# Two attention and expert layers on one core: nine rank matmuls, expert row copies three tiles ahead, stored key parts in eight buffers, and a table zeroed in long rows

## The reference, cut to what matters

```python
x = x + tanh(g_xattn[0]) * _L0_xattn_ref(_layernorm(x), ctx, ...)   # additive attention, pooled queries and keys
x = x + tanh(g_ffn[0])   * _L0_ffn_ref(_layernorm(x), ...)
x = x + tanh(g_xattn[1]) * _L1_xattn_ref(_layernorm(x), ctx, ...)   # softmax attention, 16 heads of 8
x = x + tanh(g_ffn[1])   * _L1_ffn_ref(_layernorm(x), ...)

# _L0_ffn_ref: two of eight experts for each token
logits = flat_x @ W_router + b_router
top_vals, top_idx = jax.lax.top_k(logits, TOP_K)
router_weights = jax.nn.softmax(sparse_logits, axis=-1)
for e in range(NUM_EXPERTS):
    h = jax.nn.relu(flat_x @ W1[e] + b1[e])
    y = h @ W2[e] + b2[e]
    final_output = final_output + y * w[:, None]
```

## Time and profile before

| | |
|---|---|
| time, median of 3 runs | 921.75 us (920.45 to 923.25) |
| time of the profiled execution, its span | 925.03 us, 923.3 us |
| busy: TensorE, VectorE, ScalarE, GpSimd | 58%, 50%, 29%, 42% of the span |
| mean granted TensorE clock | 0.743 |
| chain that ended last | VectorE 28%, TensorE 28%, issue 11%, unknown 11%, DMA 8% |
| first expert gather, last expert matmul of layer 0 | about 259 and 421 us |
| first and last expert matmul of layer 1 | about 779 and 894 us |

### The profile page before, as it was taken

One profiled execution on the slowest core, in us unless ns is written; L12 is line 12 of the kernel. 1 busy time (PEld: TensorE's weight loads), 2 busy tenths in 40 slices (PEclk: granted clock), 3 DMA queues, 4 the chain that ended last, 5 costly groups with the idle time before them and its releaser, 6 DMA issues.

```text
span 923.3 us, 16362 instructions
## 1 busy us (share of the span) xinstructions
PE 535.6 (58%) x4815; PEld 434.2 (47%) x4816; DVE 459.1 (50%) x1520; ACT 265.5 (29%) x442; POOL 384.9 (42%) x436
## 2 busy tenths in 40 slices
PE   2588774313069898882455566564544002999980
PEld 2256562211058777782233455443433001988870
DVE  5674686544213332234973578777785620222224
ACT  1220011201023334343511366464544100232220
POOL 5121016655115555555000245256575571555660
PEclk9786785655569999997555578577655555999995
DMA  8999999923222222211463354332114112222218
GB/s 206 247 149 171 157 149 150 131 78 99 95 58 67 68 65 65 66 55 55 112 207 111 78 146 113 86 97 48 38 42 122 36 48 62 76 73 74 70 47 278
DMA packets 108712, 94.56 MB, mean 102 GB/s; under 512 B 12344, under 2 KB 97080, under 8 KB 108584
## 3 DMA queue, kind: packets, MB, share of 16 engines
q1 hardware_dynamic: 94584, 70.04, 36.9%
q0 software_dynamic: 9840, 21.60, 8.5%
q10 hardware_dynamic: 4224, 2.10, 0.8%
HBM read 46.15 MB, written 47.45 MB: 101 GB/s over the span
## 4 chain that ended last, share of the span: by engine, by line
DVE 28%; PE 28%; issue 11%; another core or an unknown queue 11%; DMA 8%; POOL 4%; SPq 4%; ACT 3%; DVEq 2%; POOLq 0%; ACTq 0%
PE PS L698 25%; DVE work L1205 4%; DMA work<-ys 3%; DVE stats L1210 2%; DVE XN L1228 2%; DVE work L1614 2%; DVEq L1528 2%; DVE rtmp L1205 2%; DVE X L1205 2%; POOL xs L461 1%; DMA k_parts<-work 1%; DMA q_parts<-w1l 1%; DVE nwt L1221 1%; DVE work L1534 1%
## 5 line engine op out<-in xcount | busy, mean ns | idle before, releaser
L698 PE MATMUL PS<-work 128*128 128x36 f16 (+6 forms) x1376 | 109.0, 258 | 95.4 <-DVE work L1205 70.4
L472 POOL DMA_INDIRECT ys<-work x144 | 144.4, 1003 | 34.5 <-issue 34.5
L698 PE MATMUL PS<-w,work 128*128 x1152 | 145.0, 279 | 10.5 <-issue 6.4
L698 PEld LDWEIGHTS PS<-w,work 128*128 128x128 f32 x1152 | 134.2, 192 | 21.8 <-issue 20.4
L698 PEld LDWEIGHTS PS<-work 128*128 128x128 f16 (+3 forms) x1376 | 87.9, 138 | 118.4 <-issue 80.9
L1205 DVE TENSOR_TENSOR work<-PS,work 128x128 f32<-128x128 f32 (+4 forms) x130 | 51.2, 415 | 175.6 <-issue 59.8
L497 POOL TENSOR_TENSOR work<-XN,work 128x1024 f16<-128x1024 f32 x32 | 68.0, 2126 | 162.9 <-ACT work L1149 162.6
L461 POOL DMA_INDIRECT xs<-pack,adr_i x96 | 93.9, 978 | 68.7 <-ACT pack L1053 38.6
L698 PE MATMUL PS<-work,w1h 128*128 128x256 f16 x576 | 102.5, 279 | 9.9 <-DVE work L1516 8.7
L1103 ACT ACTIVATE work<-PS,b 128x256 f32<-128x256 f32 x160 | 62.7, 474 | 110.8 <-PE PS L698 96.6
L698 PE MATMUL PS<-work,w1l 128*128 128x256 f16 x288 | 80.2, 279 | 0.3 <-issue 0.3
(11 more groups left out here) (238 smaller groups left out, 840.0 us busy)
## 6 DMA issues: line engine op xcount, KB each, us to landing
xs<-zrow SPq DMA_DIRECT2D x8, 2210.0 KB
work<-xs SPq DMA_DIRECT2D x144, 65.0 KB
work<-ys SPq DMA_DIRECT2D x16, 512.0 KB, 4.4
k_parts<-work SPq DMA_DIRECT2D x24, 128.0 KB
q_parts<-w1l SPq DMA_DIRECT2D x24, 128.0 KB
w<-k_parts SPq DMA_DIRECT2D x8, 384.0 KB
work<-q_parts SPq DMA_DIRECT2D x8, 384.0 KB
work<-k_parts SPq DMA_DIRECT2D x32, 96.0 KB
```

The source lines that it names most:

```text
L472: g.indirect_dma_start(ys[l], bass.IndirectOffsetOnAxis(xin[:, q, u, :].bitcast(U32)[:, D:D + 1], 0), yrow[:, q, u, :], None).then_inc(ff[ ...
L698: return t.matmul(o, lhsT, rhs, start=start, stop=stop, skip_group_check=True)
```

## The change

**Rank:** `route_rank` covers all 8 tiles with one output of 64 columns: the running count broadcast to all, then each shift by one tile over the columns that remain, then the triangle. That makes 1 + 7 + 1 = 9 matmuls, in both layers. **Copies ahead:** a round does parts(q+3) and then result(q), in both layers; in layer 0 the expert is read before the waits, on VectorE and on ScalarE. **Key parts:** `k16` has eight buffers, at another place in the work area, and ScalarE no longer waits for stores. The stores of chunks 4 to 7 are issued behind the loads of the first eight expert tiles, and the waits for all key stores move behind experts(0), on SyncE and on ScalarE. **Zeros:** GpSimd clears 16 rows in each partition inside `w2`, and SyncE writes the table from there in 17 DMAs of 8,320 bytes for a partition. `w2` is loaded once these have landed, with its own semaphore `w2_in`, for which TensorE waits.

```diff
+ZROWS = 16
+ZPARTS = E * CAP // (P * ZROWS)
+FILLED = 16 * (ZPARTS + 1)
+AHEAD = 3
-        k16 = at(0, [2, 2, CHUNK], F16)
+        k16 = at(28, [NC, 2, CHUNK], F16)
+        zrows = w2[:, 0:ZROWS * ROW16 // 2].bitcast(F16)
...
+            g.memset(w2[:, 0:ZROWS * ROW16 // 2], 0.0).then_inc(zero, 1)
...
-            sp.dma_start(w2[:].rearrange("p (e c d) -> p e c d", e=E, c=FC),
-                         A["w2_0"].rearrange("e (c p) d -> p e c d", p=P)).then_inc(w_late, 16)
-            sp.wait_ge(zero, 1)
-            for e in range(E):
-                sp.dma_start(xs[1][e * CAP:(e + 1) * CAP, :].rearrange("(p m) n -> p m n", p=P),
-                             bc(zrow[:].bitcast(U32), 1, CAP // P)).then_inc(filled, 16)
+            sp.wait_ge(zero, 2)
+            spread = xs[1][0:E * CAP, :].rearrange("(p a m) n -> p a (m n)", p=P, m=ZROWS)
+            for part in range(ZPARTS):
+                sp.dma_start(spread[:, part, :], zrows.bitcast(U32)).then_inc(filled, 16)
...
+            sp.wait_ge(filled, FILLED)
+            sp.dma_start(w2[:].rearrange("p (e c d) -> p e c d", e=E, c=FC),
+                         A["w2_0"].rearrange("e (c p) d -> p e c d", p=P)).then_inc(w2_in, 16)
...
-            for c in range(NC // 2, NC):
-                keys_stored(c)
-            for u in range(2):
-                sp.wait_ge(qk_out[u], PART_STORES * (NC // 2))
             sp.wait_ge(tails, 16 * E)
...
-                expert_tiles(sp, l, step)
+                for q in range(XS_LEAD):
+                    step(0, q)
+                if l == 0:
+                    for c in range(NC // 2, NC):
+                        keys_stored(c)
+                with sp.Fori(1, rounds[l]) as i:
+                    for q in range(XS_LEAD):
+                        step(i, q)
...
             y_load(0, 1)
+            for u in range(2):
+                sp.wait_ge(qk_out[u], PART_STORES * (NC // 2))
...
-                t0 = pair(p).start
-                for s in range(2 * CT_TILES):
-                    o = PS[:, BANK_RANK[l], RANK0 + s * E:RANK0 + (s + 1) * E]
-                    mm(o, ones16[:], cum16[:], stop=False)
-                    for b in range(s):
-                        mm(o, ones16[:], sel16[:, t0 + b, :], start=False, stop=False)
-                    ins = mm(o, tri16[:], sel16[:, t0 + s, :], start=False)
-                ins.then_inc(rt[l]["rank"], 1)
+                sel, n = sel16[:, pair(p), :], 2 * CT_TILES
+                o = PS[:, BANK_RANK[l], RANK0:RANK0 + n * E].rearrange("p (s e) -> p s e", e=E)
+                mm(o, ones16[:], bc(cum16[:], 1, n), stop=False)
+                for back in range(1, n):
+                    mm(o[:, back:n, :], ones16[:], sel[:, 0:n - back, :], start=False, stop=False)
+                mm(o, tri16[:], sel, start=False).then_inc(rt[l]["rank"], 1)
...
-                if l == 1:
-                    pe.wait_ge(w2_in, 16)
+                pe.wait_ge(w2_in, 16 * (l + 1))
...
-                        if c >= 2:
-                            act.wait_ge(qk_out[c % 2], PART_STORES * (c // 2))
...
+                    if l == 0:
+                        e = dve.value_load(eidx_i[0:1, l, ds(i * XS_LEAD + q, 1)], min_val=0, max_val=E - 1)
                     dve.wait_ge(f["y"][v], m + 1)
...
-                def round_(i, first, last):
+                def round_(i, last):
                     for q in range(XS_LEAD):
-                        if q < XS_LEAD - 1:
-                            parts(i, q + 1)
+                        if q + AHEAD < XS_LEAD:
+                            parts(i, q + AHEAD)
                         elif not last:
-                            parts(i + 1, 0)
-                        if q >= 1:
-                            result(i, q - 1)
-                        elif not first:
-                            result(i - 1, XS_LEAD - 1)
+                            parts(i + 1, q + AHEAD - XS_LEAD)
+                        result(i, q)
```

More of the change, by code:

```diff
@@ L351, in slots @@
             return tiles(c if l == 0 else c % 4)
-        NL = 4
+        NL = 3
         NW = 8
@@ L489, in _ @@
             experts(0)
-            pool.wait_ge(filled, 16 * (E + 1))
+            pool.wait_ge(filled, FILLED)
             for step in range(NT + 16):
@@ L1078, in _ @@
                         act.wait_ge(qk_ps, c + 1)
-                        act.wait_ge(soft["pooled"], 4)
-                        if c >= 2:
-                            act.wait_ge(qk_out[c % 2], PART_STORES * (c // 2))
-                        a.activation(k16[:, c % 2, 0, :], PS[:, BANK_K[c % 2], :], ACT.Copy).then_inc(qk_hi, 1)
+                        act.wait_ge(soft["head_prod"], 4)
+                        a.activation(k16[:, c, 0, :], PS[:, BANK_K[c % 2], :], ACT.Copy).then_inc(qk_hi, 1)
                 elif step == "choose":
@@ L1096, in step @@
                     v, m = q % 2, (i + i0) * (XS_LEAD // 2) + q // 2
+                    if l == 0:
+                        e = act.value_load(eidx_i[0:1, l, ds(i * XS_LEAD + q, 1)], min_val=0, max_val=E - 1)
                     act.wait_ge(f["up"][v], m + 1)
@@ L1100, in step @@
                     if l == 0:
-                        e = act.value_load(eidx_i[0:1, l, ds(i * XS_LEAD + q, 1)], min_val=0, max_val=E - 1)
                         for c in range(FC):
@@ L1120, in blanked @@
                              bc(zrow[:, 0:2 * D], 1, HG * HG * CHUNK // (2 * D)), ACT.Copy).then_inc(s_, 1)
+            for u in range(2):
+                act.wait_ge(qk_out[u], PART_STORES * (NC // 2))
             for u in range(2):
@@ L1485, in _ @@
                         dve.wait_ge(qk_hi, c + 1)
-                        tt(k16[:, c % 2, 1, :], PS[:, BANK_K[c % 2], :], k16[:, c % 2, 0, :], ALU.subtract)\
+                        tt(k16[:, c, 1, :], PS[:, BANK_K[c % 2], :], k16[:, c, 0, :], ALU.subtract)\
                             .then_inc(qk_lo, 1)
@@ L1527, in result @@
                     if l == 0:
-                        e = dve.value_load(eidx_i[0:1, l, ds(i * XS_LEAD + q, 1)], min_val=0, max_val=E - 1)
                         tt(yrow[:, q, :, :], y, bc(b2b[:, ds(e * D, D)], 1, 2), ALU.add).then_inc(f["biased"][0], 1)
@@ L1535, in result @@
                     ins.then_inc(f["yrow"][v], 1)
-                def round_(i, first, last):
+                def round_(i, last):
                     for q in range(XS_LEAD):
-                        if q < XS_LEAD - 1:
-                            parts(i, q + 1)
+                        if q + AHEAD < XS_LEAD:
+                            parts(i, q + AHEAD)
                         elif not last:
-                            parts(i + 1, 0)
-                        if q >= 1:
-                            result(i, q - 1)
-                        elif not first:
-                            result(i - 1, XS_LEAD - 1)
+                            parts(i + 1, q + AHEAD - XS_LEAD)
+                        result(i, q)
                 rounds_ = TILES[l] // XS_LEAD
-                parts(0, 0)
-                round_(0, True, False)
+                for q in range(AHEAD):
+                    parts(0, q)
+                round_(0, False)
                 with dve.Fori(1, rounds_ - 1) as i:
-                    round_(i, False, False)
-                round_(rounds_ - 1, False, True)
-                result(rounds_ - 1, XS_LEAD - 1)
+                    round_(i, False)
+                round_(rounds_ - 1, True)
             def combine(l, c):
```

2 lines of the change are left out of this document (1 added, 1 removed).

## The result

The changed kernel takes 912.04 us (median of 20 runs, 900.38 to 922.36), the kernel before, run beside it, 921.85 us (916.87 to 925.38). The ratio is 0.985, 95% interval 0.983 to 0.987: faster by 1.5%. Either way the time lies above the range of the prediction. The profiled execution took 915.8 us, its span is 914.0 us.

The account below looks back on a forecast made before the run. Layer 0's late routing was taken as bound by key-store waits and TensorE's slow rank instructions, experts(0) by copy order. Terms -17.3 - 21.5 - 9 - 16 = -63.8 us took the 921.75 us median to 858 us; range 843 to 886.

Parts of the forecast that it names:

- Nine matmuls in stage A: Layer 0's routing: nine rank matmuls remove VectorE's three waits, -21.5 us.
- the instructions past the first eighty: TensorE's ranks: instructions past the first eighty cost, not array work; nine matmuls, 18 instructions, stay well inside.
- Rival 1: Layer 0's ranks: slow steps have another cause, say GpSimd's scatters, and nine matmuls still meet them; 879 us, chance 0.12.
- the fast 40: Layer 0's rank: the first 40 of 44 matmuls ran fast, always at the start; held against rival 1.
- Stores off the path: Between last tail and first row load: moving stores of chunks 4 to 7 saves 17.3 us, bounds -12 to -17.5.
- up to 2 us of loss: Experts(0): twelve stores behind 16 row loads, some 6.5 us, might cost up to 2 us; in the bounds, not the sum.
- Layer 1's four ranks: Layer 1's routing: nine matmuls shorten waits before its four `route_rows`, -9 us, bounds -3 and -13.
- Copies three ahead: Experts(0): earlier copies remove the wait before up and most before down, -16 us, bounds -2 and -27.
- 4.00 us a tile: Experts(0): a tile takes 4.00 us; copies ahead would make it 3.60 over 40 tiles.
- Rival 2: Experts(0): relu's output or y banks become the next wait, 3.95 us a tile; 872 us, chance 0.17.
- The same order in experts(1): Experts(1): no copy wait to remove, result stands behind one more gather; 0 us, bounds -6 and +4.
- Zeros: Early table zeroing: long rows free the DMA queues earlier but bring 0 us, bounds -3 and +2.

Follow-up runs that it names:

- slow-step batches: Batches of executions in which the kernel before, unchanged, took 921.9 and 928.7 us; the prediction's profile is of this sort.
- `after`: The changed kernel against the kernel before, first measurement and its profile: 912.04 us, ratio 0.985.
- `rank_b`: The kernel before with nine rank matmuls in place of 44 and nothing else, in a slow-step batch: ratio 0.991.
- `before_b`: The kernel before, no edit, run again in a slow-step batch: 923.7 us.
- `stores_spread`: The changed kernel with one of the twelve late key-part stores behind each row load of tiles 8 to 19, slow-step batch: 906.95 us, 0.976 of the kernel before.
- even batches: Batches of executions in which the kernel before, unchanged, took 863 to 872 us.
- `after_b`: The changed kernel, no edit, run again in a slow-step batch: 917.61 us beside 928.73 for the kernel before, ratio 0.984.
- `before_again`: The kernel before, no edit, run again in an even batch: 865.7 us.
- `zeros_only`: The kernel before with only the long-row zeros and `w2` loaded behind them, in an even batch: ratio 1.002.
- `after_again`: The changed kernel, no edit, run again in an even batch: 862.98 us beside 864.16 for the kernel before, ratio 0.999.

## Why the prediction was wrong

By its own steps, with the slow-step batches against each other, since that is what it was made from:

- **Nine matmuls in stage A, -21.5 us: wrong.** Alone they brought 6.2 us. The step that failed is "so what costs is not the array's work but the instructions past the first eighty". The slow steps belong to a stretch of time in which the next instruction of TensorE, VectorE or SyncE may be late, and not to TensorE's count. With TensorE out of the way they fall on VectorE, from 179.86 to 201.98 in `after` and from 166 to 177 in `rank_b`, and 14 to 22 of 21 to 22 us stay. Rival 1, at 0.12, had the cause (something other than the count, the scatters beside it) and the evidence for it, SyncE's slow tails. It did not have the place: it let the nine matmuls meet the slow steps, and they ran in 0.4 to 0.5 us each time. I set against it that the fast 40 always came first. They came behind a wait of TensorE each time (9.8 us, then 41 fast ones, in `before_b`); whether the wait buys them, and why, is open.
- **Stores off the path, -17.3: right** (16.0 to 17.5 from the last tail to the first row load). **But "up to 2 us of loss" behind the row loads was 6.4 us** in the slow-step batch (183.7 against 177.3 with the stores spread) and 13 in the even ones (167.7 against 154.7). The twelve took 14.5 us and not 6.5: I priced them by stores that had waits between them, and put none of them against its neighbour.
- **Layer 1's four ranks, -9: wrong**, for the same reason as the first. The stage got 0.7 and 3.0 us shorter in two pairs of profiles; the bound was -3.
- **Copies three ahead, -16: wrong.** VectorE's copy is no longer waited for (7.7 to 1.4 us), and in `stores_spread`, where the ninth tile is in time, the stage is 1.6 to 4.4 us shorter than before. The step that failed took 4.00 us a tile for a matter of order. In even batches the old order runs at TensorE's pace; with the late releases it takes 4.00. That they then find the next wait is read from the profiles of the whole change, since the copies were not run alone in a slow-step batch. Rival 2 had the size (2 us of 16 left to the copies).
- **The same order in experts(1), 0 (at most +4): wrong in size.** 5.3 and 7.0 us longer in slow-step batches, 0.4 shorter in the even one. `rank_b`, with the old order, keeps 129.5 us, and `stores_spread`, with the new one, takes 135.6. The traces name the wait. In 102 us of experts(1) TensorE waits 2.5 us for gelu's output before and 1.2 in `before_b`, but 4.9 in `after_b` and 7.0 in `after`:

```profile
PE PS L708 <- ACT work L1112: 7.0, 9, 1.0
```
- **Zeros, 0: right.** 1.002 alone. The rule of the Trainium skill against which it was weighed (DMA: Bandwidth & Descriptors, section Specifications: full rate from 512 bytes) doesn't hold for this transfer. With the 8,320-byte rows DMA moved 366 and 422 GB/s, with the 520-byte rows 166. The faster zeros changed no term all the same: in `before_again` the chain does run through the issue of the short rows until 172.9 us, and without them (`zeros_only`) the stage is only 1.6 us shorter.

In `after` the first row load is 18.7 us earlier, the first load of results 11.9 (434.8 to 422.9), the last one 10.0. So experts(0) took 7 us back, layer 1's scatters gave 3 and experts(1) took 5. The range was too narrow because three of the four large terms rested on one reading of one execution's slow steps. They failed together, and a single rival with 0.12, which moved two of them, stood for that.

## What to carry to other kernels

An engine that is late for no reason that the profile names ("issue", an unknown queue) should not be priced as that engine's instruction count until a second engine has been looked at in the same stretch: if its steps are late too, taking work off one hands the delay to the other. Before a wait is priced, find what stands next behind it on every queue (here GpSimd's 64 scatters, for which SyncE waits 11.8 us in `after_again`). Stores that are moved off a path want a gap for each: twelve in a row took 15 to 20 us wherever they were put, one in a tile took 0.6 us each and brought a further 0.8 to 1.5%.

## What the hardware did that was not expected

- The same program takes 863 to 872 us in some batches and 922 to 929 in others, with the granted clock alike (0.743 and 0.750 in the two profiles) and no matmul or scatter longer (0.97 us for a scatter in both). Some 60 us are late instructions and releases, and they stand in the four stages in which GpSimd issues indirect DMAs all along. The cause is open.
- Twelve 128 KB stores in a row: on SyncE's queue 0.5 to 0.8 us for each of the first five, then up to 2.7; on ScalarE's 0.5 to 1.4 and then up to 3.2. And the last scatter beside them landed in 6.5 to 6.7 in place of 2.3 us.
- A memset of 1.84 us on GpSimd makes VectorE's 0.34 us `tensor_scalar` 1.83 us.
